# First attention and first FFN merged into one block of a four-stage transformer kernel

## What is computed

```
x = x + tanh(g_xattn[0]) * attention_0(layernorm(x), ctx, ctx)   # 16 heads of 8
x = x + tanh(g_ffn[0])   * ffn_0(layernorm(x))     # dense: expert chosen by position
x = x + tanh(g_xattn[1]) * attention_1(layernorm(x), ctx, ctx)   # 16 heads of 64
x = x + tanh(g_ffn[1])   * ffn_1(layernorm(x))     # each token to its argmax expert of 8

def ffn_0(x):
    xn = layernorm(x) * ln_scale + ln_bias
    xa = xn @ attn_w.T + attn_b + x
    h  = gelu(xa per group of 256 tokens @ w1[e] + b1[e])
    return gelu((h @ w2[e] + b2[e]) @ next_w.T + next_b)
```

## Time and profile before

| | |
|---|---|
| median of 3 runs | 782.08 us |
| the three runs | 780.7, 782.08, 782.43 us |
| the profiled execution's own time | 779.87 us |
| its span, first to last instruction | 778.1 us |
| busy in the span: PE, DVE, ACT, POOL | 744.4, 609.9, 545.1, 458.2 us |
| mean granted clock of PE | 0.982 of full |

### The profile page before, as it was taken

One profiled execution on the slowest core, in us unless ns is written; L12 is line 12 of the kernel. 1 busy time (PEld: TensorE's weight loads), 2 busy tenths in 40 slices (PEclk: granted clock), 3 DMA queues, 4 the chain that ended last, 5 costly groups with the idle time before them and its releaser, 6 DMA issues.

```text
span 778.1 us, 29664 instructions
## 1 busy us (share of the span) xinstructions
PE 744.4 (96%) x10488; PEld 621.2 (80%) x10489; DVE 609.9 (78%) x2369; ACT 545.1 (70%) x1101; POOL 458.2 (59%) x863
## 2 busy tenths in 40 slices
PE   5899999999899999999999999999999999999994
PEld 2688888887788868888888888888888888788883
DVE  5799999998677747787888888888889888785452
ACT  2588888886555578777777777777767777666662
POOL 5455777873022426576776767677666677427553
PEclk8699999999999999999999999999999999999998
DMA  8903999900200000000000000000000100003210
GB/s 247 304 3 123 280 269 231 230 4 3 76 1 0 1 1 3 2 8 7 0 7 7 7 7 0 7 7 7 3 4 7 32 25 0 9 8 101 70 31 12
DMA packets 56323, 41.72 MB, mean 54 GB/s; under 512 B 3929, under 2 KB 51811, under 8 KB 56016
## 3 DMA queue, kind: packets, MB, share of 16 engines
q1 hardware_dynamic: 52848, 36.53, 17.9%
q0 software_dynamic: 2272, 4.27, 1.7%
q10 hardware_dynamic: 1152, 0.27, 0.2%
HBM read 18.07 MB, written 23.44 MB: 53 GB/s over the span
## 4 chain that ended last, share of the span: by engine, by line
PE 67%; DVE 4%; issue 1%; ACT 1%; POOL 0%; DVEq 0%; POOLq 0%; ACTq 0%
PE f_bank L2069 15%; PE f_bank L56 13%; PE fold_bank L56 12%; PE fold_bank L2035 5%; PE fold_bank L959 4%; PE f_bank L965 4%; PE f_bank L1179 3%; PE fold_bank L2030 2%; PE fold_bank L1170 2%; PE fold_bank L2013 1%; PE f_bank L970 1%; PE f_bank L947 1%; PE f_bank L954 1%; DVE x_sb L1413 1%; DVE l_neg_max L1390 1%
## 5 line engine op out<-in xcount | busy, mean ns | idle before, releaser
L2069 PE MATMUL f_bank<-l_Z,l_probs 128*128 128x129 f32 x1024 | 165.4, 285 | 1.6 <-ACT l_probs L1867 0.9
L2069 PEld LDWEIGHTS f_bank<-l_Z,l_probs 128*128 128x128 f32 x1024 | 138.5, 191 | 20.9 <-DVE l_acc L1413 4.4
L1800 POOL TENSOR_TENSOR l_qk_lo<-w,l_qk_hi 128x512 f16<-128x512 f32 x128 | 144.4, 1158 | 15.4 <-ACT l_qk_hi L1882 14.7
L1413 DVE SCALAR_TENSOR_TENSOR x_sb<-f_bank,l_inv,x_sb 128x128 f32 (+1 forms) x256 | 89.8, 351 | 30.6 <-DVE l_inv L1400 5.5
L1867 ACT ACTIVATE l_probs<-fold_bank 128x512 f32<-128x512 f32 x128 | 72.7, 595 | 52.7 <-PE fold_bank L2035 52.6
L56 PE MATMUL fold_bank<-M,cT 128*128 128x512 f16 x384 | 104.1, 380 | 3.8 <-DVE l_T_lo L1384 2.9
L1857 ACT ACTIVATE w<-f_bank 128x512 f32<-128x512 f32 x124 | 74.0, 597 | 41.2 <-PE f_bank L56 39.4
L505 DVE TENSOR_REDUCE n_shared<-fold_bank 128x4 f32<-128x512 f32 x128 | 87.3, 682 | 11.2 <-PE fold_bank L742 8.6
L1872 ACT ACTIVATE l_Z<-fold_bank 128x512 f32<-128x512 f32 x124 | 74.2, 599 | 7.2 <-PE fold_bank L56 3.6
L1861 ACT ACTIVATE l_qk_hi<-w 128x512 f16<-128x512 f32 x124 | 77.4, 624 | 1.0
L1413 DVE SCALAR_TENSOR_TENSOR l_acc<-f_bank,l_inv,l_acc 128x128 f32<-128x128 f32 x224 | 76.7, 342 | 0.1
(11 more groups left out here) (311 smaller groups left out, 2313.6 us busy)
## 6 DMA issues: line engine op xcount, KB each, us to landing
expert_rows<-empty_row SPq DMA_DIRECT2D x8, 2178.0 KB, 23.8
x_sb<-expert_rows SPq DMA_DIRECT2D x39, 66.0 KB, 1.9
w<-in_L_ffn_w SPq DMA_DIRECT2D x1, 2048.0 KB, 9.3
x_sb<-in_x SPq DMA_DIRECT2D x3, 512.0 KB, 7.3
ctx_sb<-in_ctx SPq DMA_DIRECT2D x3, 512.0 KB, 8.4
w_raw<-in_L_ffn_gate_w SPq DMA_DIRECT2D x1, 1408.0 KB, 11.7
w_raw<-in_L_ffn_up_w SPq DMA_DIRECT2D x1, 1408.0 KB, 11.5
downT<-in_L_ffn_down_w SPq DMA_DIRECT2D x2, 512.0 KB, 4.3
```

What stands on the lines that cost most here:

```text
L1413: nc.vector.scalar_tensor_tensor(out=total, in0=O[:, h, 0:P], scalar=inv[:, j:j + 1], in1=total, op0=ALU.mult, op1=ALU.add).then_inc(summe ...
L1800: nc.gpsimd.tensor_tensor(qk_lo[:, w, m, Q * u:Q * u + Q].rearrange("p t n -> p (t n)"), qk[:, u, m, :], qk_hi[:, w, m, Q * u:Q * u + Q].r ...
L2069: last = nc.tensor.matmul(pv_bank[m % 2][:, h * (P + 1):(h + 1) * (P + 1)], probs[:, 2 * m + h, :], Z[:, w, 2 * m + h, :], start=True, sto ...
```

## The change

The block of the first attention is gone. `first_attention` now returns five functions, one for each engine, and the last block's lists call them first. All eight PSUM banks are taken once, as `k.fold_bank` and `k.other_bank`; the first attention and the first FFN use the same ones. The first pair's FFN work is written among steps B-1 to B+2 of the first attention, and the eight `keep_awake` matmuls are gone. Since M is now written earlier, batch 31's probabilities lie elsewhere, in `w_raw`. The l1 tensors `probs` and `rowsT`, where that work is put, are allocated first. The down weights' load waits until all of x is added. In the second FFN, the tiles from 12 on write their result to two banks in turn, and POOL's tiny addition moves ahead of the wait for the first result. The diff is cut to its core, and without the lines that only move to the left:

```diff
-def first_attention(nc, A, k):
+def first_attention(nc, ctx, outer, A, k):
...
+    last_probs = k.w_raw[:, 2 * R * 512:3 * R * 512].rearrange("p (r n) -> p r n", r=R)
+
+    def probs_of(n, s):
+        return last_probs if isinstance(n, int) and n == B - 1 else probs[s % 2]
...
-        *a_bank, stack_bank, front_bank = k.fold_bank
-        b_bank = [ctx.enter_context(nc.psum_tensor(f"l0_b{n}", [P, 512], F32)) for n in range(2)]
-        misc_bank, sum_bank = (...)
+    stack_bank, front_bank, *b_bank = k.fold_bank
+    *a_bank, sum_bank, misc_bank = k.other_bank
...
# vector, in step()
+            if isinstance(n, int) and n == B:
+                f0.transposed(dve, 0)
+            if isinstance(n, int) and n == B + 1:
+                folded_lo(dve, 2)
...
-                        if n in (B - 1, B):
-                            k.norms.statistics(dve, n - B + 3, (n - B + 3) % 2)
-                        if n > B:
-                            k.folded_lo(dve, n - B - 1)
+                if n == B - 1:
+                    k.norms.statistics(dve, 2, 0)
+                    f0.vector_begin(dve)
+                if n == B:
+                    for part in range(2):
+                        folded_lo(dve, part)
+                    f0.attended(dve, 0)
+                if n == B + 1:
+                    folded_lo(dve, 3)
+                    f0.transposed(dve, 1)
+                if n == B + 2:
+                    k.norms.normalised(dve, 2, 0)
+                    k.norms.statistics(dve, 3, 1)
...
# scalar, in step(): the first part ahead of sums_out(n - 1), the second at the step's end
+            if isinstance(n, int) and n == B:
+                f0.scalar_begin(act)
+                for part in (0, 1):
+                    folded_hi(part)
...
+            if isinstance(n, int) and n == B + 1:
+                for part in (2, 3):
+                    folded_hi(part)
...
-                for n in range(4):
-                    act.wait_ge(k.folded, n // 2 + 1)
-                    nc.scalar.activation(k.M_hi[:, there(n), :], ...)
...
# tensor, in step()
+            if isinstance(n, int) and n == B + 2:
+                f0.first_product(pe, 0, (0, 1), fresh=True)
                     if live(-3):
                         project_heads(n - 3)
+            if isinstance(n, int) and n == B + 1:
+                f0.attend(pe, 0, back=False)
+                pe.wait_ge(exp_done, R * B + R)
+                fold(1)
+            if isinstance(n, int) and n == B + 2:
+                f0.first_product(pe, 0, (2, 3), fresh=True)
...
                     if live(-2):
                         transpose_sums(n - 2)
                     if isinstance(n, int) and n == B:
+                pe.wait_ge(max_ready, R * B)
+                f0.tensor_begin(pe)
                         pe.wait_ge(k.late_landed, 16 * 2)
+                pe.wait_ge(x_done, B - 2)
+                pe.wait_ge(V_ready, B)
                         fold(0)
                     if isinstance(n, int) and n == B + 1:
-                        fold(1)
+                f0.transpose(pe, 1)
...
# FirstFfn
-    def first_product(self, pe, g):
+    def first_product(self, pe, g, some=range(H0), fresh=False):
         pe.wait_ge(self.xa_ready, g + 1)
-        for c in range(H0):
+        for c in some:
+            if fresh:
+                pe.wait_ge(self.k.M_lo_ready, c + 1)
...
     def next_product(self, pe, g):
         pe.wait_ge(self.eo_ready, g + 1)
+        if g == 0:
+            pe.wait_ge(self.k.first_added, B)
...
     def tensor_begin(self, pe):
...
-        keep_awake(nc, k, self.eo_bank, 3)
         self.transpose(pe, 0)
-        keep_awake(nc, k, self.eo_bank, 4)
-        self.attend(pe, 0, back=False)
-        self.transpose(pe, 1)
-        keep_awake(nc, k, self.eo_bank, 1)
-        self.first_product(pe, 0)
...
# SecondFfn
+    def out_place(self, n):
+        return self.out_bank[n % 2][:, 0:P] if n >= EARLY else self.out_bank[0][:, 0:P]
...
             pool.wait_ge(self.token_ready, i + 1)
-            for v in range(U):
-                pool.wait_ge(self.result_ready, U * i + v + 1)
-                if v == 0:
                     pool.wait_ge(self.taker_ready, i + 1)
                     nc.gpsimd.tensor_tensor(self.taker[:, 1:2], ...)
+            for v in range(U):
+                pool.wait_ge(self.result_ready, U * i + v + 1)
...
         if n:
-            pe.wait_ge(self.result_ready, n)
+            pe.wait_ge(self.result_ready, n - 1 if n > EARLY else n)
...
# second_attention
-        ffn.banks(tz_bank, pv_bank[0], (qk_bank, a_bank[0]), (a_bank[1], b_bank[0]), b_bank[1])
+        ffn.banks(tz_bank, pv_bank, (qk_bank, a_bank[0]), (a_bank[1], b_bank[0]), b_bank[1])
...
             def _(sp):
+                first_sync(sp)
+                sp.wait_ge(k.first_added, B)
                 f0.load(sp, A)
```

More of the change, by code:

```diff
@@ new lines, in sb, with sem @@
+    def sb(name, shape, dt=F32):
+        return ctx.enter_context(nc.sbuf_tensor("l0_" + name, shape, dt))
+    def sem(name):
+        return outer.enter_context(nc.semaphore("l0_" + name))
+    carrier = sb("carrier", [P, 3])
+    taker = sb("taker", [P, 2])
+    bn = sb("bn", [P, 2, 6])
+    stats = sb("stats", [P, 2, 2])
+    work = sb("work", [P, 2, 4])
+    xn = k.norms.shared[:, 0]
+    bias_row = sb("bias_row", [P, P])
+    T_hi = sb("T_hi", [P, P], F16)
+    T_lo = sb("T_lo", [P, P], F16)
@@ new lines, in probs_of @@
+    def probs_of(n, s):
+        return last_probs if isinstance(n, int) and n == B - 1 else probs[s % 2]
+    sums = k.downT[:, 2].rearrange("p e n -> p (e n)")[:, 0:4 * P]
+    inv = sb("inv", [P, H])
+    heads_out, headsT = (k.norms.shared[:, 0, w, 1, :] for w in range(2))
+    stack_bank, front_bank, *b_bank = k.fold_bank
+    *a_bank, sum_bank, misc_bank = k.other_bank
+    names = ("primed bn_done stats_ready norm_step xn_ready cT_hi_ready cT_ready bias_added T_moved T_hi_ready T_lo_ready qk_done qk_hi_ready "
+             "qk_lo_ready v_done V_ready q_stacked k_stacked stack_q stack_k scored max_ready maxT_moved maxT_ready shifted "
+             "exp_done pv_done sums_ready sums_moved inv_ready heads_ready heads_moved headsT_ready projected x_done tokens_landed w_hi_ready").split()
@@ new lines, in row, with every_step, there @@
+    def row(t, n):
+        return t[:, bass.ds(n, 1), 0:P].rearrange("p a n -> p (a n)")
+    def every_step(engine, step):
+        for n in range(FIRST, DEEP * LOOP[0]):
+            step(n, n, lambda ahead, n=n: 0 <= n + ahead < B)
+        with engine.Fori(*LOOP) as i:
+            for s in range(DEEP):
+                step(DEEP * i + s, DEEP * LOOP[0] + s, lambda ahead: True)
+        for n in range(DEEP * LOOP[1], LAST):
+            step(n, n, lambda ahead, n=n: 0 <= n + ahead < B)
+    def there(n):
+        return slice(4 * n, 4 * n + 4)
@@ L862, in __init__ @@
         self.outT = sb("outT", [P, 2 * P])
-        self.t_bank, self.attn_bank, self.eo_bank, self.next_bank = (ctx.enter_context(nc.psum_tensor(f"f0_bank{n}", [P, 512], F32)) for n in range(4))
+        self.t_bank, self.attn_bank, self.eo_bank, self.next_bank = k.other_bank
         self.hid_bank = k.fold_bank
@@ L1224, in sem @@
             return ctx.enter_context(nc.semaphore("l1_" + name))
+        probs = sb("probs", [P, H, P])
+        rowsT = sb("rowsT", [P, 2, P])
         carrier = sb("carrier", [P, 3])
```

803 lines of the change are left out of this document (381 added, 422 removed).

## The result

| | before | changed |
|---|---|---|
| median of the runs | 780.88 us (6 runs, 779.63 to 782.43) | 774.50 us (6 runs, 772.44 to 776.05) |
| ratio, 95% interval | | 0.9917 (0.9902 to 0.9933) |
| profiled execution: own time, span | 779.87, 778.1 us | 775.62, 773.6 us |
| from the last scatter's start to the span's end | 8.67 us | 8.43 us |

The change makes the kernel 6.5 us faster (5.2 to 7.7). The prediction said 4.9 us faster, 777.2 us with a range from 775.2: right in direction, too small in size.

The account below looks back on a forecast made before the run. PE was taken to bound the kernel, with time lost at the handover and POOL's scatters at the end. Handover 4.43 plus tail 0.49 made 4.92 us, off the median 782.08: 777.2 us, range 775.2 to 779.4.

Parts of the forecast that it names:

- The handover's work and order: From sums of batch 30 to pair 0's second product: 8.39 us of PE work plus 0.45 wait, 4.43 us earlier.
- M_lo part 3: At the handover, DVE finishes it by 198.7 us, just before PE's fourth chunk of the first product wants it at 198.9.
- The table load: In ACT's queue at the handover, its 1.28 us is hidden, with 0.9 us to spare.
- The prediction's sum by the skill: With 1.38 us drain, ACT's copy comes about 195.9, PE waits some 0.3 us, and the gain is 4.1.
- The tail: Last tiles of the second FFN: a second result bank and POOL's earlier addition bring the last scatter 0.49 us forward.
- The price of the old handover: Sums of batch 30 to pair 0's second product took 13.26 us in the profiled execution before the change.
- rival C: Raised for a rerun of the changed kernel: its low clock at the start ends earlier, by 1 us or more on average.
- The base: The 4.92 us gain was taken off the median of before, 782.08 us, not the profiled execution's 779.87.
- Rival 2: At the handover PE's clock falls without fillers; half speed for 19 us loses 9.5, giving 786.7 us; chance 0.04.
- Rival 1: DVE becomes the bound at the handover, PE loses 1 to 2 us, giving 778.7 with 1.5; chance 0.11.
- Rivals 3 and 4: 3: changed banks or addresses slow attention steps, 780.0 us, chance 0.05; 4: later stages give time back, near 782, 0.04.

Follow-up runs that it names:

- one_block_old_order: Changed kernel's one block, shared banks and new tail, without fillers, but pair 0's first steps behind the first attention's last ones; ratio to before 0.9998, handover 14.66 us.
- tail_only: Kernel before with only the second FFN's tail changed: two result banks and POOL's addition first; ratio to before 1.0000.
- after_again: The changed kernel run again, unchanged, beside the kernel before; ratio 0.9925 (0.9903 to 0.9947).

## Why the prediction was wrong in size and right in its mechanism

- **The handover's work and order: right.** 8.39 us of work and one wait were predicted, 8.83; 8.73 came. The wait was 0.24 instead of 0.45. M_lo part 3, the narrowest place, did not hold PE.
- **The table load: right by the trace.** ACT's next real activation starts 0.11 us behind the tiny one. The Trainium skill (ScalarE: Activation LUTs, section What ACT_TABLE_LOAD costs) states about 1.38 us of drain beside the load. The rows above do not show it: ACT's last exponential ends 0.02 us before the load (191.40 + 1.08, and 192.50), and the tiny activation starts 0.01 us behind the load's 1.28. The prediction's sum by the skill, the copy of sums 31 at about 195.9, leaves out the tiny activation's 0.20 that its own walk has; with it the copy would end at 196.1 and PE wait 0.5.
- **The tail: right in size**, 0.55 for 0.49, and the argument held: the three scatters move only if the first one does. That it takes both parts of the change was shown by the two kernels with one of them.
- **The price of the old handover: the step that failed.** The prediction took 13.26 us from one execution and subtracted it from the median of all. That execution was, as the text said, 2.21 us below the median; the text chose the base by it, but did not ask whether the handover was short in it too. In four of six profiles of that order the handover is 14.6, since PE's clock falls behind the pause at the barrier. By the rows, the gain is 5.0 to 5.3 us where the clock holds and 1.3 more where it falls. With four of six it is 5.9 to 6.2, inside the measured 5.7 to 7.1, and 5.0 to 5.3 is outside. That the old handover is longer in most profiles is shown; that this makes up the missing 1.5 us is only the likeliest account, since filling the pause gained nothing in a median, and the start (rival C above) could carry some of it.
- **The base.** The median of before went from 782.08 (3 runs) to 780.88 (6 runs), so 1.2 of the 2.7 us by which the time was missed is the base's. The other 1.5 is the gain: 4.9 predicted, 6.4 measured. The range reached 2.0 us below the forecast, of which the text explains 1.2 ("mostly the spread of the three runs", and up to 0.4 in the tail), and had nothing for a price read from a lucky execution.
- **Rival 2 was the right mechanism on the wrong kernel.** It asked whether the change would let the clock fall, and took the 1.00 of the earlier trace rows for the state of the kernel before; in most profiles it fell there, fillers or not. The changed order has no pause over 0.24 us there, and the clock was at 1.00 in nine of nine profiles. The Trainium skill (TensorE: Matmul & The Clock Gate, Part 4: PE-mode transpose) states that a transpose doesn't count as PE-busy the same way as a matmul. The prediction made of it that the clock would drop in a handover "with more transposes", but both orders have the same transposes and only the fillers are gone; the nine profiles show no drop, and between the transposes stand folds and products, so they don't test the statement itself.
- **Rival 1** (DVE becomes the bound) did not come, though DVE was full from 198 to 202 us. **Rivals 3 and 4** did not come. For the attention's steps (rival 3): from the transposes of sums at 99.78 us to those at 190.54 before it is 90.76 us, and 90.74 after (100.87 to 191.61), so the 1.07 us by which the changed profile was later arose before 101 us. For the rest: the regular FFN step is 5.02 us, and pair 0's second product to the last hidden transposes is 561.58 us for 561.83.

## What to carry to other kernels

A wait that a barrier shows belongs to the work behind it: look at what the late engine has queued before you count the barrier as a gain, since merging the blocks without moving that work gained nothing here. Before a stretch's duration is taken off a median, ask whether the profiled execution was typical in it, above all where PE pauses over a microsecond: the clock behind the pause may differ from one execution to the next, and the range has to hold both.

## What was not expected of the hardware

- A pause of PE of 1.3 to 1.5 us was followed by 1.2 GHz for some 3 us in four of six executions of one order, and the clock held in the other two. The instructions around it are the same.
- At the start, twice the clock for 15 us moved the first attention's end by 2.8 us between two profiles on one chip and hardly the median. The DMA engines' share is 1.0 or more there.
- One block in place of two shortens the end of the span by 0.24 us and lengthens the time outside the span by 0.3 (1.74 to 2.06); one_block_old_order has both, tail_only neither.
- On the chips with medians of before of 788 us and more the second FFN takes 5 to 7 us longer in both kernels (83 to 85 us for 77.5 from its first hidden transposes to its last). Between 700 and 720 us PE, DVE and ACT all pause there, and PE's clock falls to 0.50 behind it in ten of twelve profiles. From DVE's timeline of after_again:

```profile
702.94 0.35 DVE L1080 SCALAR_TENSOR_TENSOR w<-other_bank,tg,x_sb 128x128 f32<-128x128 f32 x1 [3.42 <-remote]
707.25 0.52 DVE L1070 TENSOR_TENSOR w<-fold_bank,w 128x352 f32<-128x352 f32 x1 [3.96 <-remote]
```

  What they wait for there was not tried.
